# Block counts on ScalarE beside VectorE's histogram, and the first ranks made two blocks at a time

## Chip, cores and metric

The kernel runs on one core of a Trainium2 chip. The metric is the device time of one execution in microseconds (us). Before the change it is 6723.85 us, the median of 3 runs (6722.99 to 6726.43).

## What is computed

Four graph layers over one graph of 6250 nodes and 100000 edges, each followed by a residual and a layer norm:

```python
edge_index = jnp.stack([src, dst])
x = _layernorm(x + _L0_gnn_ref(x, edge_index, ...), axis=-1)      # two hops, then two matrices
x = _layernorm(x + _L1_gnn_ref(x, edge_index, ...), axis=-1)      # hypergraph convolution
x = _layernorm(x + _L2_gnn_ref(x, edge_weight, src, dst), axis=-1)
x = _layernorm(x + _L3_gnn_ref(x, edge_index, edge_attr_64, ...), axis=-1)   # attention over edges
```

The change touches only what comes ahead of the layers: the kernel counts the edges of each destination node (for `deg`) and sorts the edges by the block of their source node. There are 49 blocks of 128 nodes (`NB` = 49). For each edge its rank in that order is needed, and for this the number of edges of each source block in each of the 128 partitions (`cnt`).

## The kernel before

The program is a row of phases. Each phase (`phase`, L66) is a block in which the five engines run side by side, ordered by semaphores, and it ends with a barrier of all engines. What a phase takes is so what its slowest engine takes. The first three phases matter here.

**prepare** (L118). SyncE's queue loads the edge lists, the node rows and the weights, then fills the table `bucketed_edges` in HBM with 52 transfers of 544 KB (L158). VectorE makes the index tables. `m.shi` is the source block of each of the 784 edges that a partition holds; its name in the trace is `start_t`. Then comes a loop of 49 iterations (L278). An iteration first counts one source block: L280 compares all 784 values of `shi` with the block's number and adds up the hits into one column of `m.cnt`. Then it makes the one-hot rows of 16 edge columns in two halves of 8: L285 the high part of the destination (one instruction for 8 columns), L289 the low part (one for each column). TensorE adds them up as a histogram in PSUM (L328). After the loop VectorE makes `deg` (L293), ScalarE its root (L175), VectorE the reciprocal (L295) and the scaled node rows (L298), which SyncE's queue stores (L161). This store and the fill of L158 must have landed before the phase ends.

**starts** (L767, `bucket_starts`). TensorE sums `cnt` over the partitions (L798, L799). VectorE makes from it where each block starts, and then the ranks of the first 112 edge columns of each partition (`CHUNKS[1]` = 7 * 16) in `rank_columns` (L749). It takes the 49 blocks one after the other: a mask (L756), a running sum over it that starts at the block's present position in each partition, `m.first` (L758), a copy of the sum to `m.rank` where the mask holds (L760), and a copy of its last column back to `m.first` (L761). Each of them waits for the one that it reads from, and the iteration's last wait is for all four.

**bucket** (L806). GpSimd scatters the edges by their ranks (L863, 784 indirect DMAs), 16 columns at a time. ScalarE makes the indices (L844) and copies three values for each edge (L847); it may begin with the first 112 columns at once and waits for the further ranks, which VectorE makes meanwhile with `rank_columns` for 224 and 448 columns. Then VectorE makes a second histogram, with the same shapes as the first one but without a count (L881, L885, L898).

`hold` (L87) is a wait followed by a NOP.

Of the kernel before, what the change touches and what calls it, by code (L numbers as in the profile page):

```python
# [7 lines left out]
I32 = mybir.dt.int32  # L8
ALU = mybir.AluOpType
# [4 lines left out]
P = 128  # L14
N, D = 6250, 128
E, DE = 100000, 64
M = 2500
# [5 lines left out]
NT = NI * U  # L23
# [37 lines left out]
assert Q3 == 2 * G and U3 // G % RG == 0  # L61
assert NI == NB
assert (P - 1) * NT + SPLIT * U == E and 0 < SPLIT < NI
assert M <= KW <= NB * P and (NB - 1) % CR == 0 and (NB - 1) % 2 == 0 and 3 * NB * NR <= BT and NB % GB == 0 and NPC % RING == 0 and NCH == MB


class Names:
# [47 lines left out]
def prepare(nc, m, a):  # L115
# [7 lines left out]
    whole, rest = (P - 1) * NT, E - (P - 1) * NT  # L123
    with phase(nc, "prepare", "filled loaded_edges loaded_rows counted loaded_x loaded_w iota dve hw_row consts nat transposed evacuated "
                              "diag replicated rep_used span_ready wT wT_used prefilled fill hist_ready "
                              "hist_used degree root scaled stored") as (S, block):
        FT = (CH - 1) * P
        LT = FULL - FT

# [36 lines left out]
        @block.scalar  # L166
        def _(act):
            act.dma_start(m.hwrow[:, 0:M], a.hw.rearrange("(o n) -> o n", o=1).broadcast_to([P, M])).then_inc(S["hw_row"], 16)
            act.wait_ge(S["hw_row"], 16)

            for k, dst in enumerate((m.w1T, m.w2T, m.WT)):
                act.wait_ge(S["wT"], k + 1)
                nc.scalar.copy(dst[:, :], m.ps[:, 4 + k, 0:P]).then_inc(S["wT_used"], 1)
            act.wait_ge(S["degree"], 1)
            nc.scalar.activation(m.dinv[:, :], m.deg[:, :], ACT.Sqrt).then_inc(S["root"], 1)  # L175

# [12 lines left out]
        def _(v):  # L189
# [80 lines left out]
            step(V.tensor_copy(m.dst2, rowI[1]))  # L270
            step(V.tensor_scalar(m.shigh, m.dst2, float(M), PAD, ALU.is_lt, ALU.mult))
            step(V.tensor_tensor(m.shigh, m.shigh, m.shi, ALU.add))

            v.wait_ge(S["hw_row"], 16)
            step(V.memset(m.hwrow[:, M:KW], 0.0))
            step(V.memset(m.side[:, NP:AW], 0.0))

            with v.Fori(0, NI) as i:  # L278
                b = bass.ds(i, 1)
                V.tensor_scalar(m.tabs[:, 0:NT], m.shi, m.iota[:, b], None, ALU.is_equal, ALU.add, accum_out=m.cnt[:, b]).then_inc(S["counted"], 1)  # L280
                for h in range(2):

                    v.wait_ge(S["hist_used"], i * 2 + h + 1)
                    cols = bass.ds(i * U + h * HALF, HALF)
                    V.tensor_tensor(m.ohhi[:, h * HALF:(h + 1) * HALF, :],  # L285
                                    m.dhi[:, cols].unsqueeze(2).to_broadcast([P, HALF, NB]),
                                    m.iota[:, 0:NB].unsqueeze(1).to_broadcast([P, HALF, NB]), ALU.is_equal).then_inc(S["hist_ready"], 1)
                    for k in range(HALF):
                        V.tensor_scalar(m.ohlo[:, h * HALF + k, :], m.iotab[:, :], m.dlo[:, bass.ds(i * U + h * HALF + k, 1)],  # L289
                                        None, ALU.is_equal).then_inc(S["hist_ready"], 1)  # L290
                v.wait_ge(S["counted"], i + 1)
            v.wait_ge(S["hist_used"], 2 * NI + 3)
            V.tensor_scalar(m.deg[:, :], m.ps[:, 7, 0:NB], 1.0, None, ALU.add).then_inc(S["degree"], 1)  # L293
            v.wait_ge(S["root"], 1)
# [467 lines left out]
        v.wait_ge(S["ranked"], i * 4 + (done * 4 * NB + 4))  # L762


def bucket_starts(nc, m):


    with phase(nc, "starts", "dve cnt_in_psum ends ends_in_psum ranked") as (S, block):
        @block.vector
        def _(v):  # L770
            V, step = nc.vector, chain(v, S["dve"])
            v.wait_ge(S["cnt_in_psum"], 2)

            step(V.tensor_copy(m.bI[:, :], m.ps[:, 0, 0:NB]))
            step(V.tensor_scalar(m.bF[:, :], m.bI[:, :], float(P - 1), None, ALU.add))
            step(V.tensor_copy(m.bI[:, :], m.bF[:, :]))
            step(V.tensor_scalar(m.bI[:, :], m.bI[:, :], 7, None, ALU.arith_shift_right))
            step(V.tensor_copy(m.bF[:, :], m.bI[:, :]))
            step(V.tensor_tensor_scan(m.ends[:, :], m.ones[:, 0:1].to_broadcast([P, NB]), m.bF[:, :], 0.0, ALU.mult, ALU.add))
            step(V.tensor_tensor(m.bF[:, :], m.ends[:, :], m.bF[:, :], ALU.subtract))  # L780
            step(V.tensor_copy(m.fac[:, :], m.bF[:, :]))
            step(V.tensor_scalar(m.bF[:, :], m.bF[:, :], float(P), -1.0, ALU.mult, ALU.add))
            step(V.tensor_tensor(m.first[:, :], m.bF[:, :], m.ps[:, 1, 0:NB], ALU.add))

            for col, u, sh in ((2, U, 4),):
                step(V.tensor_scalar(m.small[0:1, col:col + 1], m.ends[0:1, NB - 1:NB], float(u - 1), None, ALU.add))
                step(V.tensor_copy(m.smallI[0:1, col:col + 1], m.small[0:1, col:col + 1]))
                step(V.tensor_scalar(m.smallI[0:1, col:col + 1], m.smallI[0:1, col:col + 1], sh, None, ALU.arith_shift_right))
            V.tensor_copy(m.bF[:, :], m.ends[:, :]).then_inc(S["ends"], 1)
            v.wait_ge(S["ends_in_psum"], 2)  # L790
            step(V.tensor_copy(m.bstart[0:NB, :], m.ps[0:NB, 3, 0:1]))
            step(V.tensor_copy(m.endp[0:NB, :], m.ps[0:NB, 2, 0:1]))
            step(V.tensor_scalar(m.rank[:, :], m.tF[:, 0:NT], float(DUMP), None, ALU.add))
            rank_columns(nc, v, m, S, 0, 0)

        @block.tensor
        def _(pe):
# [946 lines left out]
```

## Time and profile before

| | |
|---|---|
| time, median of 3 runs | 6723.85 us |
| time of the profiled execution | 6730.24 us |
| its span in the trace | 6728.5 us |
| TensorE busy | 4012.2 us (60%) |
| VectorE busy | 3279.4 us (49%) |
| GpSimd busy | 3044.2 us (45%) |
| ScalarE busy | 1187.3 us (18%) |
| prepare | to about 356 us |
| starts | about 356 to 446 us |
| bucket begins | 446.8 us |

The busy shares are means over some thirty phases. Since every phase ends in a barrier, they tell little of one phase: which engine or transfer ends it must be read from its own stretch of the trace.

### The profile page before, as it was taken

To read this page: it belongs to the slowest core of one execution; us is meant where nothing else is said; L and a number is where in the kernel's file an instruction comes from. 1 tells how busy PE (TensorE), PEld (TensorE's weight loads), DVE (VectorE), ACT (ScalarE), POOL (GpSimd) and SP (SyncE) were. 2 spreads that over 40 slices of the span, in tenths; PEclk is the share of its full clock that TensorE was granted. 3 is DMA by queue.
4 is the path that set the end of the run, shared out by engine and by line. 5 is a ranking of instruction groups with operands and counts; after the bars stand their busy time and mean duration, and the time that the engine had idled before them with its cause. 6 is when DMAs were issued, how large, how long until landed. Compare 5 with 4: busy or idle time off the path is not lost. (4 is left out here: it accounts for less than half of the span.)

```text
span 6728.5 us, 101449 instructions
## 1 busy us (share of the span) xinstructions
PE 4012.2 (60%) x17222; PEld 2420.5 (36%) x17251; DVE 3279.4 (49%) x11280; ACT 1187.3 (18%) x3845; POOL 3044.2 (45%) x3024
## 2 busy tenths in 40 slices
PE   2600510002676777876877999566666567777777
PEld 1300300000111112434454456343443357666665
DVE  5967920003555555443122033544444557788783
ACT  0000000000111110001012022100000156666652
POOL 0027877770000003874750000377777447777750
PEclk9999999999656557888975999555555589999995
DMA  8611112217111114655732856111111234444450
GB/s 128 88 37 48 40 50 54 54 51 23 70 62 70 62 70 157 204 178 173 258 107 100 311 192 199 44 53 52 53 52 53 46 108 130 125 126 127 124 103 19
DMA packets 717405, 673.00 MB, mean 100 GB/s; under 512 B 487624, under 2 KB 616377, under 8 KB 698166
## 3 DMA queue, kind: packets, MB, share of 16 engines
q1 hardware_dynamic: 607526, 442.47, 23.8%
q0 software_dynamic: 109568, 227.77, 12.2%
q14 instruction: 152, 1.25, 0.1%
q10 hardware_dynamic: 144, 1.28, 0.1%
q8 instruction: 15, 0.25, 0.0%
HBM read 528.30 MB, written 142.96 MB: 100 GB/s over the span
## 5 line engine op out<-in xcount | busy, mean ns | idle before, releaser
L488 POOL DMA_INDIRECT gathered<-node_table,idx x576 | 621.3, 1079 | 1174.9 <-ACT idx L476 1015.5
L863 POOL DMA_INDIRECT bucketed_edges<-edge_rows,idx x784 | 822.9, 1050 | 681.6 <-issue 663.3
L1329 POOL DMA_INDIRECT gathered<-node_table_xq,idx x832 | 798.5, 960 | 377.3 <-issue 225.0
L360 POOL DMA_INDIRECT gathered<-node_table,idx x816 | 771.0, 945 | 285.4 <-issue 203.3
L375 PE MATMUL ps<-onehots,gathered 128*128 128x128 f32 x1632 | 642.5, 500 | 422.0 <-DMA gathered<-node_table,idx 421.4
L1239 PE MATMUL ps<-onehots 128*128 128x512 bf16 x1152 | 573.3, 571 | 263.6 <-DVE onehots L1266 253.6
L435 PE MATMUL ps<-gathered,junk 128*128 128x512 f32 x1182 | 608.1, 623 | 90.2 <-DMA gathered<-edge_counts 90.0
L375 PEld LDWEIGHTS ps<-onehots,gathered 128*128 128x128 f32 x1632 | 408.1, 312 | 656.4 <-DMA gathered<-node_table,idx 656.1
L1157 PE MATMUL ps<-tabs,ones 49*128 49x416 f32 x4 | 3.1, 938 | 707.1 <-DVE tabs L1112 707.1
L1264 DVE TENSOR_SCALAR onehots<-iota_b,side_rows,bF 128x128 bf16<-128x128 bf16 x722 | 227.2, 315 | 396.9 <-issue 207.3
L971 POOL MEMSET agg<- 128x6400 f32 x4 | 21.7, 5432 | 848.5 <-ACTq L81 848.5
L1418 PE MATMUL ps<-Wh,attend_slots 128*128 128x128 f32 x1664 | 357.7, 299 | 47.8 <-issue 44.1
L504 PEld LDWEIGHTS ps<-onehots,gathered 128*128 128x128 f32 x1152 | 223.2, 210 | 446.0 <-DMA gathered<-node_table,idx 251.5
L539 DVE TENSOR_TENSOR onehots<-ps,off_t 128x512 f32<-128x512 f32 x156 | 107.2, 691 | 534.0 <-PE ps L504 530.5
L1239 PEld LDWEIGHTS ps<-onehots 128*128 128x128 bf16 x1152 | 90.6, 108 | 731.0 <-DVE onehots L1266 729.2
L504 PE MATMUL ps<-onehots,gathered 128*128 128x128 f32 x1152 | 264.4, 316 | 145.6 <-DMA gathered<-node_table,idx 141.2
L1112 DVE TENSOR_SCALAR tabs<-tile_iota_i,endp 49x832 f32<-49x832 f32 x1 | 0.6, 645 | 706.2 <-PEq L84 706.2
L1419 PE MATMUL ps<-side_rows,attend_slots 128*128 x1664 | 343.1, 290 | 0.0
L393 DVE TENSOR_TENSOR onehots<-ps,off_t 128x512 f32<-128x512 f32 x208 | 143.9, 692 | 400.1 <-PE ps L375 400.0
L1266 DVE TENSOR_SCALAR onehots<-junk,side_rows 128x1024 bf16<-128x1024 f16 (+1 forms) x722 | 312.2, 432 | 30.0
L1218 ACT COPY gathered<-ps 128x512 f32<-128x512 f32 x245 | 133.9, 588 | 971.4 <-PE ps L1242 971.4
L898 PE MATMUL ps<-gathered 128*128 128x49 bf16 x784 | 123.5, 222 | 304.2 <-DVE gathered L885 294.0
(358 smaller groups left out, 7719.2 us busy)
## 6 DMA issues: line engine op xcount, KB each, us to landing
gathered<-edge_counts SPq DMA_DIRECT2D x99, 1280.0 KB
edge_counts<-gathered SPq DMA_DIRECT2D x49, 1280.0 KB
gathered<-edge_counts SPq DMA_DIRECT2D x56, 896.0 KB
bucketed_edges<-edge_rows SPq DMA_DIRECT2D x52, 544.0 KB, 12.1
edge_rows<-bucketed_edges SPq DMA_DIRECT2D x208, 128.0 KB
gathered<-edge_counts SPq DMA_DIRECT2D x48, 512.0 KB
side_rows<-edge_counts SPq DMA_DIRECT2D x48, 512.0 KB
gathered<-node_table,idx POOLq DMA_INDIRECT x1392
```

Source lines behind the costliest of these rows:

```text
L360: nc.gpsimd.indirect_dma_start(g[:, k, :], None, table, bass.IndirectOffsetOnAxis(m.idx[:, k:k + 1], 0)).then_inc(S["landed"][k], 16)
L375: last = nc.tensor.matmul(m.ps[:, q, e * P:(e + 1) * P], g[:, k, :], m.oh[:, k, :], start=True, stop=True)
L435: mm = nc.tensor.matmul(m.ps[:, k, :], m.junk[:, j, :], row_piece(m, j, k), start=first, stop=False)
L488: nc.gpsimd.indirect_dma_start(g[:, k, :], None, a.table, bass.IndirectOffsetOnAxis(m.idx[:, k:k + 1], 0)).then_inc(S["landed"][k], 16)
L504: last = nc.tensor.matmul(sums[q % NS], g[:, k, :], m.oh[:, k, :], start=e == 0, stop=e == G - 1)
L863: nc.gpsimd.indirect_dma_start(a.bucketed, bass.IndirectOffsetOnAxis(m.idx[:, k:k + 1], 0), m.erow[:, k, :], None).then_inc(S["scattered"] ...
L1239: last = T.matmul(m.ps[:, k, :], ohs[h], ohd[h][:, (k - k0) * KB:(k - k0 + 1) * KB], start=False, stop=False)
L1264: V.tensor_scalar(ohs[h], m.iotab[:, :], m.meta[:, bass.ds(t + h, 1), 2], m.bF[:, bass.ds(b, 1)], ALU.subtract, ALU.is_equal)
L1266: V.tensor_scalar(ohd[h][:, 0:w], iotaK[:, 0:w], m.meta[:, bass.ds(t + h, 1), 1], -float(k0 * KB), ALU.subtract, ALU.is_equal).then_inc(S[ ...
L1329: nc.gpsimd.indirect_dma_start(g[:, k, :], None, a.table2, bass.IndirectOffsetOnAxis(m.idx[:, k:k + 1], 0)).then_inc(S["landed"][s], 16)
L1418: T.matmul(out, m.eT[:, 2 * h + e // 2, :], m.Wh[:, e % 2, :], start=True, stop=False)
L1419: last = T.matmul(out, m.ohT[:, G * h + e, :], m.side[:, bass.ds(start[e], P)], start=False, stop=True)
```

## The change

ScalarE makes the 49 counts, in two passes for each block over one of two buffers in `m.side`: the square of (block number minus `shi`), which is 0 where the edge belongs to the block and at least 1 elsewhere, and then Relu(1 - square), whose sum is the count. It starts when `shi` is there (the new semaphore `blocks`). The count and its wait leave VectorE's loop. In the phase starts, the first 112 columns' ranks are made for two blocks in one iteration: two masks, two running sums, then copy and `first` for the one and the other, in two buffers each; the 49th block is left for the end. The ranks of the later parts are as before.

```diff
+            act.wait_ge(S["blocks"], 1)
+            act.sem_inc(S["counted"], 2)
+            apart = [m.side[:, k * NT:(k + 1) * NT] for k in range(2)]
+            with act.Fori(0, NB // 7) as i:
+                b0 = act.snap(i * 7)
+                for j in range(8):
+                    if j < 7:
+                        act.wait_ge(S["counted"], b0 + max(j + 1, 2))
+                        nc.scalar.activation(apart[j % 2], m.shi, ACT.Square, scale=-1.0, bias=m.iota[:, bass.ds(b0 + j, 1)]).then_inc(S["apart"], 1)
+                    if j >= 1:
+                        act.wait_ge(S["apart"], b0 + j)
+                        nc.scalar.activation(apart[(j - 1) % 2], apart[(j - 1) % 2], ACT.Relu, scale=-1.0, bias=m.ones[:, 0:1],
+                                             accum_out=m.cnt[:, bass.ds(b0 + (j - 1), 1)]).then_inc(S["counted"], 1)
+            act.wait_ge(S["counted"], NB + 2)
             act.wait_ge(S["degree"], 1)
             nc.scalar.activation(m.dinv[:, :], m.deg[:, :], ACT.Sqrt).then_inc(S["root"], 1)
...
             step(V.tensor_tensor(m.shigh, m.shigh, m.shi, ALU.add))
+            v.sem_inc(S["blocks"], 1)
...
             with v.Fori(0, NI) as i:
-                b = bass.ds(i, 1)
-                V.tensor_scalar(m.tabs[:, 0:NT], m.shi, m.iota[:, b], None, ALU.is_equal, ALU.add, accum_out=m.cnt[:, b]).then_inc(S["counted"], 1)
                 for h in range(2):
...
-                v.wait_ge(S["counted"], i + 1)
...
+def rank_columns_by_two(nc, v, m, S):
+
+    V, n = nc.vector, CHUNKS[1]
+    mask, cum = ([t[:, k * n:(k + 1) * n] for k in range(2)] for t in (m.tabs, m.cum))
+
+    def ranks(b0, count, base):
+        b = [bass.ds(b0 + k, 1) for k in range(count)]
+        for k in range(count):
+            V.tensor_scalar(mask[k], m.shi[:, 0:n], m.iota[:, b[k]], None, ALU.is_equal).then_inc(S["ranked"], 1)
+        for k in range(count):
+            hold(v, S["ranked"], base + (k + 1))
+            V.tensor_tensor_scan(cum[k], m.ones[:, 0:1].to_broadcast([P, n]), mask[k], m.first[:, b[k]], ALU.mult, ALU.add).then_inc(S["ranked"], 1)
+        for k in range(count):
+            hold(v, S["ranked"], base + (count + 1 if k == 0 else 2 * count + 1))
+            V.copy_predicated(m.rank[:, 0:n], mask[k].bitcast(I32), cum[k]).then_inc(S["ranked"], 1)
+            V.tensor_copy(m.first[:, b[k]], cum[k][:, n - 1:n]).then_inc(S["ranked"], 1)
+        v.wait_ge(S["ranked"], base + 4 * count)
+    with v.Fori(0, NB // 2) as i:
+        ranks(v.snap(i * 2), 2, v.snap(i * 8))
+    ranks(NB - 1, 1, 4 * (NB - 1))
...
-            rank_columns(nc, v, m, S, 0, 0)
+            rank_columns_by_two(nc, v, m, S)
```

In the instruction lists that follow, ISA, REGISTER_ALU and the branches belong to the sequencer; a semaphore in brackets is waited for ahead of that row. Semaphores that a later phase takes over keep the name of their first owner.

ScalarE in prepare, from the copies of the transposed weights to the root of `deg`, before:

```order
L173 ACT_TABLE_LOAD [waits prepare_wT]
L173 COPY w1T<-ps 128x128 [waits prepare_hw_row]
L173 COPY w2T<-ps 128x128 [waits prepare_wT]
L173 COPY WT<-ps 128x128 [waits prepare_wT]
L175 ACT_TABLE_LOAD
L175 ACTIVATE dinv<-deg 128x49 [waits prepare_degree]
```

And now, the end of the new loop over 7 blocks and what follows it:

```order
L182 ISA [waits prepare_counted]
L182 ACTIVATE side_rows<-start_t,iota 128x784
L184 ISA
L185 ISA [waits prepare_apart]
L185 ACTIVATE side_rows,cnt<-side_rows,ones 128x784
L184 ISA
L185 ISA [waits prepare_apart]
L185 ACTIVATE side_rows,cnt<-side_rows,ones 128x784
L177 REGISTER_ALU
L177 COMPARE_AND_BRANCH
L189 ACT_TABLE_LOAD [waits prepare_degree]
L189 ACTIVATE dinv<-deg 128x49 [waits prepare_counted]
```

The loop holds activations alone; the load of the table for the root stands behind it, and it now carries the wait for `deg`, which the root alone carried before.

VectorE in starts, the loop over the 49 blocks, before:

```order
L754 ISA
L756 TENSOR_SCALAR tabs<-start_t,iota 128x112
L757 ISA
L758 ISA [waits prepare_loaded_x]
L758 SCALAR_TENSOR_TENSOR gathered<-ones,first,tabs 128x112
L89 ISA
L760 COPY_PREDICATED rank_t<-tabs,gathered 128x112 [waits prepare_loaded_x]
L761 ISA
L761 COPY first<-gathered 128x1
L762 ISA
L754 REGISTER_ALU [waits prepare_loaded_x]
L754 COMPARE_AND_BRANCH
```

And now, the same loop over 24 pairs, up to the first block's copies:

```order
L785 TENSOR_SCALAR tabs<-start_t,iota 128x112
L785 ISA
L785 TENSOR_SCALAR tabs<-start_t,iota 128x112
L89 ISA
L788 ISA [waits prepare_loaded_x]
L788 SCALAR_TENSOR_TENSOR gathered<-ones,first,tabs 128x112
L89 ISA
L788 ISA [waits prepare_loaded_x]
L788 SCALAR_TENSOR_TENSOR gathered<-ones,first,tabs 128x112
L89 ISA
L791 COPY_PREDICATED rank_t<-tabs,gathered 128x112 [waits prepare_loaded_x]
L792 ISA
```

Behind each mask there was its own running sum and nothing else to do meanwhile; now the other block's mask or sum stands between a sum and its copy. What follows in the loop, not shown, is the copy to `first` of the first block, the two copies of the second block (L791, L792) behind one more hold, and the wait for all eight.

## Rows read from the trace of the kernel before

**Rows 1.** Windows: us; PE, PEld, DVE, ACT, POOL busy; PEclk, DMA share, GB/s

```profile
280.00:300.00 20.00, 11.52 (x69) 7.01 (x68) 20.00 (x88) 0.00 (x0) 0.00 (x0) 1.00 0.00 0
...
343.00:356.00 13.00, 0.00 (x0) 0.00 (x0) 0.00 (x0) 0.00 (x0) 0.00 (x0) 1.00 0.86 247
```

**Rows 2.** Timeline of prepare's loop, VectorE: start us, us, instruction, xcount

```profile
122.05 1.03 DVE L280 TENSOR_SCALAR_CACHE_REDUCE tabs<-start_t,iota 128x784 f32<-128x784 f32 x1
...
122.99 0.57 DVE L285 TENSOR_TENSOR gathered<-gathered,iota 128x392 bf16<-128x392 f32 x1
123.47 1.39 DVE L289 TENSOR_SCALAR gathered<-iota_b,gathered 128x128 bf16<-128x128 bf16 x8
...
126.55 1.03 DVE L280 TENSOR_SCALAR_CACHE_REDUCE tabs<-start_t,iota 128x784 f32<-128x784 f32 x1
```

**Rows 3.** Sources of both histogram loops: ns min/median/max, first to last start

```profile
L280 DVE TENSOR_SCALAR_CACHE_REDUCE tabs<-start_t,iota x49: 1025/1031/1033, 113.0 to 329.4; 128x784 f32<-128x784 f32 x49
L289 DVE TENSOR_SCALAR gathered<-iota_b,gathered x784: 250/257/259, 114.5 to 333.8; 128x128 bf16<-128x128 bf16 x196
L881 DVE TENSOR_TENSOR gathered<-ew_t,iota x98: 552/564/581, 700.0 to 872.6; 128x392 bf16<-128x392 f32 x98
L885 DVE TENSOR_SCALAR gathered<-iota_b,off_t x784: 238/255/493, 700.5 to 874.3; 128x128 bf16<-128x128 bf16 x196
```

**Rows 4.** Timeline of prepare's end: start us, us, instruction, [idle before, releaser]

```profile
334.56 0.21 DVE L293 TENSOR_SCALAR deg<-ps 128x49 f32<-128x49 f32 x1 [0.53 <-PE ps L332]
334.80 0.24 ACT L175 ACTIVATE dinv<-deg 128x49 f32<-128x49 f32 x1 [251.15 <-DVE deg L293]
...
342.52 0.37 SPq L161 DMA_DIRECT2D node_table<-t_nodes  x1
```

**Rows 5.** Source L158, the fill: issue ns min/median/max, first to last start

```profile
L158 SPq DMA_DIRECT2D bucketed_edges<-edge_rows x52: 399/3552/4394, 78.3 to 256.7; - x52
```

**Rows 6.** Groups of ScalarE by form: us busy, mean ns of one, idle before

```profile
L1364 ACT ACTIVATE attend_slots<-junk,ones 128x512 bf16<-128x512 f32 x208 | 150.1, 721 | 23.0
L1084 ACT ACTIVATE gathered<-x_nodes 128x3200 f32<-128x3200 f32 x4 | 11.5, 2869 | 2.6 <-DVE x_nodes L1065 2.6
L1084 ACT ACTIVATE gathered<-x_nodes 128x3072 f32<-128x3072 f32 x4 | 11.1, 2762 | 41.1 <-DVE x_nodes L1065 41.1
L1380 ACT ACTIVATION_READ_ACCUMULATOR probs<-scores,negm 128x1 f32 x104 | 19.4, 187 | 0.0
```

**Rows 7.** Timeline of ScalarE at a table load: start us, us

```profile
5463.20 1.28 ACT L1379 ACT_TABLE_LOAD   x1
5464.50 0.20 ACT L1379 ACTIVATE c<-dif 128x1 f32<-128x1 f32 x1
```

**Rows 8.** Timeline of VectorE in starts: one block's ranks, the next mask

```profile
363.99 0.28 DVE L756 TENSOR_SCALAR tabs<-start_t,iota 128x112 f32<-128x112 f32 x1 [0.44 <-DVE first L761]
364.40 0.45 DVE L758 TENSOR_TENSOR_SCAN gathered<-ones,first,tabs 128x112 f32<-128x112 f32 x1
364.95 0.28 DVE L760 COPY_PREDICATED rank_t<-tabs,gathered 128x112 f32<-128x112 int32 x1
365.15 0.15 DVE L761 COPY first<-gathered 128x1 f32 x1
365.71 0.28 DVE L756 TENSOR_SCALAR tabs<-start_t,iota 128x112 f32<-128x112 f32 x1 [0.41 <-DVE first L761]
```

**Rows 9.** Source L761 in starts; ScalarE's waits: us in total, times, longest

```profile
L761 DVE COPY first<-gathered x49: 146/147/150, 363.4 to 445.8; 128x1 f32 x49
ACT idx L844 <- DMA bucketed_edges<-edge_rows,idx: 1006.4, 96, 15.8
...
ACT idx L844 <- PEq L84: 111.8, 1, 111.8
```

**Rows 10.** Windows of later phases, columns as in rows 1

```profile
1820.00:1980.00 160.00, 112.75 (x267) 23.03 (x270) 89.27 (x239) 21.13 (x39) 0.00 (x0) 0.57 0.16 66
...
4060.00:4220.00 160.00, 160.00 (x773) 103.95 (x773) 48.74 (x83) 40.95 (x70) 0.00 (x0) 1.00 0.55 180
```

More of the change, by code:

```diff
@@ L63 @@
 assert (P - 1) * NT + SPLIT * U == E and 0 < SPLIT < NI
-assert M <= KW <= NB * P and (NB - 1) % CR == 0 and (NB - 1) % 2 == 0 and 3 * NB * NR <= BT and NB % GB == 0 and NPC % RING == 0 and NCH == MB
+assert M <= KW <= NB * P and (NB - 1) % CR == 0 and (NB - 1) % 2 == 0 and 3 * NB * NR <= BT and NB % 7 == 0 and 2 * CHUNKS[1] <= NT and NB % GB == 0 and NPC % RING == 0 and NCH == MB
 class Names:
@@ L125, in prepare @@
                               "diag replicated rep_used span_ready wT wT_used prefilled fill hist_ready "
-                              "hist_used degree root scaled stored") as (S, block):
+                              "hist_used degree root scaled stored blocks apart") as (S, block):
         FT = (CH - 1) * P
```

## Prediction, made before the changed kernel ran

> **What bounds the kernel here.** The whole-kernel shares say little, so I began with the windows over the first 446 us, then read the groups by source line, the timelines of the loops, and the waits.
>
> In prepare, VectorE is busy for every microsecond of the histogram loop while ScalarE does nothing and TensorE is busy for 58% [rows 1]. The loop is VectorE's: each of 49 iterations lasts 4.50 us (122.05 to 126.55), and 0.94 us of it (122.05 to 122.99) passes between the start of the count and that of the next instruction [rows 2]. Behind the loop hangs a chain with one engine at a time: `deg`, root, reciprocal, scaled rows, and the store of L161 from 342.52 [rows 4]. The only other thing that this phase waits for is the fill of `bucketed_edges`: its last transfer is issued at 256.7 [rows 5], and from 280 to 300 us the DMA engines move nothing [rows 1].
>
> In starts, the ranks of part 0 are a chain on VectorE alone. Blocks follow each other at 1.72 us (363.99 to 365.71) [rows 8], and the last one's copy starts at 445.8 [rows 9]. The bucket phase begins at the barrier behind it: that is ScalarE's single wait of 111.8 us ahead of L844. Later ScalarE waits at L844 only for scattered edges, never for ranks [rows 9].
>
> So both edits work on stretches that nothing else covers, with a barrier behind each, and what they save is saved at the end, unless something else in prepare is uncovered or a later stage answers to the shift.
>
> **The counts.** Removed from VectorE: 49 counts. The price is measured twice. By the timeline, 0.94 to 0.95 us each. By a loop that stands in the same trace without the count, in the bucket phase, with the same shapes: 174.3 us from its first start to its last (700.0 to 874.3) against 220.8 us for prepare's (113.0 to 333.8) [rows 3]. The difference is **46.5 us**, and it already holds the branch, the register work and TensorE's pace. The wait on `counted` costs nothing in either.
>
> Added on ScalarE: 98 passes over 784 columns. No such shape is in the trace. From 512 columns (721 ns) and 0.84 ns for each further column (107 ns for 128 more, 2762 to 2869) a pass is 0.95 us, and reading the sum is 0.19 us [rows 6]. A block is then 2.09 us; with 0.1 us for the wait of a pass for the one before, 2.2 us. 49 of these are 108 us: from about 113 us, when the loop starts, to 221. VectorE's loop would end at 113.0 + 174.6 = 287.6, so 67 us of cover are left, and I cost this at nothing. If the cover were gone, each microsecond of ScalarE behind 287.6 would be one of the kernel. The bounds for a block: 1.9 us (each pass overlapping the next by 0.09) and 3.1 us (half as slow again); neither reaches the cover's end.
>
> The fill: it must land before the phase ends, and it has about 20 us in hand. The store of L161 would start at 342.5 - 46.5 + 1.3 = 297.3, behind the last fill, whose engines are idle from 280 at the latest. It costs nothing, but the reserve is used: a further 30 us taken from VectorE here would be partly lost.
>
> The table load: before, ScalarE loaded the root's table at leisure. Now the load stands behind the loop, and it, not the root, carries the wait for `deg`. It falls into the chain of [rows 4]. The one load inside a run of work goes from 5463.20 to the next start at 5464.50 [rows 7], so **+1.3 us**. Bounds: 0 (if the load runs ahead of the wait after all) and 2.6 (paid twice). The Trainium skill, "ScalarE: Activation LUTs", What ACT_TABLE_LOAD costs, adds a drain of about 1380 ns to the 1283 ns of the load, 2.66 us in all. By that the sum would be 1.4 us smaller in its gain. The row shows 1.30 us from start to start with no drain behind or ahead, and the sum goes by the row.
>
> **The ranks.** One block today: mask to sum 0.41 us, sum to copy 0.55, copy to `first` 0.20, `first` to the next mask 0.56, together 1.72 [rows 8]. Three of these steps hold a wait for the instruction just before (0.13, 0.10 and 0.41 us of idling). The third, copy to `first`, holds none: there the second starts 0.20 us after the first, which lasts 0.28; they overlap by nearly 0.09 us. Now a pair, from its first mask: second mask at 0.20; first sum at 0.41 (it waits for the first mask alone, as today); second sum at 0.82, halfway between the 0.77 of an overlap and the 0.86 of none, since no row shows a sum followed without a wait; first copy at 1.18 and its `first` at 1.37; the second copy waits for the first to be done, 0.38 behind its start, 1.56; its `first` at 1.75; next mask 0.56 later, at 2.31. Two blocks today are 3.43 (48 steps at 1.717, from 363.40 to 445.8, make 82.4 us [rows 9]). That is 1.13 us for each pair, and 24 pairs give **27 us**. The 49th block stays as it is. Bounds: 10 us if only the loop's idle 0.41 us is saved once in each pair (24 x 0.41), 31 us if the sums overlap and the second copy has no wait of its own. I take 27, since each of its steps but one has a row.
>
> **Sum.** -46.5 + 1.3 - 27 = -72.2 us. The profiled execution took 6730.24 us (span 6728.5 and 1.7 around it), so it would take 6658.0. It stands 6.4 us above the median of the runs, 6723.85, and the median moves to about 6651.6; I say 6652, which is 1.1% less. About 0.2% (13.4 us) is what a measurement of this kernel can tell from no change.
>
> **Rivals.**
> *No overlap on VectorE.* If an instruction starts only when the one before has left the engine, a pair is: second mask at 0.28, first sum 0.56, second 1.01, first copy 1.46, `first` 1.74, second copy 1.89, `first` 2.17, next mask 2.73. That saves 0.70 x 24 = 17 us, and the time is 6662. The Trainium skill, "VectorE: DVE Perf Modes", The DRAIN you can't avoid, says of chained operations that the next does not start until the pipe empties, semaphores or not; by that rule pairing buys only the waits. The step from copy to `first` speaks against it (0.20 us behind an instruction of 0.28) [rows 8]; the untested sum speaks for some of it. Chance 0.14.
>
> *Only the loop's idling is saved.* Holds and register work in front of each new instruction eat the rest; 10 us in place of 27, 6669. The hold in front of today's copy costs 0.10 us all told, which speaks against it. Chance 0.04.
>
> *Slower: the clock.* Later phases answer to TensorE's clock, which was granted at 0.57 on the average in the count phase (between the levels of 1.2 and 2.4 GHz) and at 1.00 in the stretch from 4060 to 4220 us, in which TensorE is busy all the time [rows 10]. All of this comes 72 us earlier now, behind a shorter and denser start. If the grant of that busy stretch and the like one before it, 320 us, fell to half for more than 86 us, the change would be slower; if for half of them, the time is 6652 + 160 = 6812. For it: the level has fallen elsewhere under less work. Against it: three runs within 3.4 us, and the histogram's density is that of the bucket phase, which ran at 1.00. A shift by some 10 us either way is as likely as not, and the range has room for it. Chance of a slower kernel 0.03.
>
> *The counts don't hide.* If each of the 98 passes brought a table load of 1.30 us, a block would be 4.8 us and ScalarE done at 113 + 235 = 348, 60 us behind VectorE's loop: 6712, no measurable change. It decides from 3.6 us a block, and gives all back at 5.0. The instruction list has one load, behind the loop. Chance 0.02.
>
> **Chances and range.** The forecast 0.77, no overlap 0.14, idling alone 0.04, slower clock 0.03, counts uncovered 0.02. Faster 0.95, same 0.02, slower 0.03. The range goes from 6639 (27 turned to 31, and 9 us for the later stages) to 6672 (10 us from the ranks, the load at 2.6, and 2 of the later stages): it takes in the first two rivals and leaves the others out.
>
> **What the profile after would show.** Right: the first one-hot to the last in prepare at about 174 us; ScalarE busy in it for about 100 us and done near 221; a table load of 1.28 us between `deg` and the root; ranks of part 0 stepping by 2.3 us a pair; the bucket phase beginning at 446.8 - 72 = 374.6; GpSimd's scatter as long as before. Wrong: a VectorE loop over 176 us (ScalarE in its way), a ScalarE end behind 287, a pair over 2.6 us, DMA still busy with the fill when the store starts, or later phases longer than before by more than some microseconds.

## The result, and the profile of the changed kernel

| | median (lowest to highest) us, runs |
|---|---|
| before, in the same series | 6727.2 (6721.93 to 6770.42), 12 |
| changed | 6695.95 (6679.31 to 6727.43), 12 |
| ratio, 95% interval | 0.9948 [0.9926, 0.9971] |
| profiled execution of the changed kernel | 6687.46, span 6685.7 |
| forecast | 6652 (6639 to 6672) |

The changed kernel is faster, by 31 us between the medians and 35 by the ratio. The forecast was 72, and its range did not hold the time. About half of the expected gain is missing. I first looked for it where the gain should arise.

The sources of prepare's two loops and of the ranks, changed kernel (ns min/median/max, first to last start):

```profile
L182 ACT ACTIVATE side_rows<-start_t,iota x49: 932/948/950, 112.4 to 206.7; 128x784 f32<-128x784 f32 x49
L185 ACT ACTIVATE side_rows<-side_rows,ones x49: 931/932/935, 114.1 to 208.5; 128x784 f32<-128x784 f32 x49
L185 ACT ACTIVATION_READ_ACCUMULATOR side_rows<-side_rows,ones x49: 184/186/189, 114.9 to 209.3; - x49
L298 DVE TENSOR_TENSOR gathered<-gathered,iota x98: 553/560/571, 112.8 to 285.3; 128x392 bf16<-128x392 f32 x98
L302 DVE TENSOR_SCALAR gathered<-iota_b,gathered x784: 242/249/259, 113.3 to 287.0; 128x128 bf16<-128x128 bf16 x196
L792 DVE COPY first<-gathered x49: 140/146/148, 318.1 to 376.1; 128x1 f32 x48, 128x1 f32<-128x1 f32 x1
```

VectorE's histogram goes from 112.8 to 287.0, 174.2 us where it was 220.8 [rows 3]. ScalarE needs 2.0 us a block and is done at 209.5, with 78 us in hand. The ranks' last copies span 58.0 us (318.1 to 376.1) where they spanned 82.4 [rows 9].

The end of prepare, timeline (start us, us, instruction, idle before and its releaser), answering to [rows 4]:

```profile
287.74 0.21 DVE L305 TENSOR_SCALAR deg<-ps 128x49 f32<-128x49 f32 x1 [0.53 <-PE ps L344]
288.03 1.28 ACT L189 ACT_TABLE_LOAD   x1 [78.53 <-DVE deg L305]
289.32 0.24 ACT L189 ACTIVATE dinv<-deg 128x49 f32<-128x49 f32 x1
...
297.04 0.37 SPq L161 DMA_DIRECT2D node_table<-t_nodes  x1
```

`deg` comes 46.8 us earlier, the table load waits for it and takes 1.3 us on the path, and the store starts 45.5 us earlier. The fill is not in its way: from 260 to 280 us the DMA engines are busy for 23% (it was issued by 257.7).

One pair of ranks on VectorE, timeline, answering to [rows 8] (x2 is two instructions shown as one):

```profile
321.97 0.47 DVE L785 TENSOR_SCALAR tabs<-start_t,iota 128x112 f32<-128x112 f32 x2 [0.55 <-DVE first L792]
322.45 0.79 DVE L788 TENSOR_TENSOR_SCAN gathered<-ones,first,tabs 128x112 f32<-128x112 f32 x2
323.16 0.26 DVE L791 COPY_PREDICATED rank_t<-tabs,gathered 128x112 f32<-128x112 int32 x1
323.33 0.14 DVE L792 COPY first<-gathered 128x1 f32 x1
323.53 0.29 DVE L791 COPY_PREDICATED rank_t<-tabs,gathered 128x112 f32<-128x112 int32 x1
323.72 0.15 DVE L792 COPY first<-gathered 128x1 f32 x1
324.40 0.47 DVE L785 TENSOR_SCALAR tabs<-start_t,iota 128x112 f32<-128x112 f32 x2 [0.54 <-DVE first L792]
```

A pair takes 2.43 us where 2.31 was forecast. The two sums, with no wait between them, take 0.79 us together though one alone takes 0.45: they overlap, as the step from copy to `first` had it. What came out longer is the stretch from `first` to the next mask, 0.54 us idle in place of 0.41. That this is a matter of the loop's place, and not of the term, shows below.

So the front part did what was forecast, but for 2.5 us. What comes behind it did not. Below, how much earlier (-) or later (+) a place is reached than in the profiled execution of before, for the kernel changed and the experiments that follow. "Scatter" is the start of the last scatter of the bucket phase (1512.0 in before), "count" the first and last matmul of the count phase (1633.5, 2598.1) and "attention" the first and last start of ScalarE's 128x128 pass there (5445.7, 6527.6).

| kernel | `deg` | bucket begins | scatter | count first | count last | attention first | last | end |
|---|---|---|---|---|---|---|---|---|
| changed | -46.8 | -69.7 | -69.2 | -69.1 | -58.1 | -57.5 | -43.4 | -42.8 |
| e1 changed again | -46.6 | -69.4 | -62.9 | -63.0 | -51.8 | -49.8 | -3.7 | -1.4 |
| e2 counts only | -46.5 | -45.1 | -42.2 | -42.2 | -42.3 | -41.1 | -21.1 | -20.8 |
| e3 ranks only | -0.1 | -24.3 | -24.6 | -24.6 | -13.4 | -20.7 | -7.8 | -6.9 |
| e4 changed, delayed | -46.4 | +16.5 | +36.2 | +36.5 | +34.2 | +47.0 | +15.1 | +14.7 |
| e5 changed + 94 | -46.4 | -72.1 | -59.7 | -59.5 | -61.8 | -61.7 | -95.4 | -93.8 |
| e6 before + 109 | +0.3 | +0.3 | +16.2 | +16.3 | +14.0 | +19.7 | -12.1 | -12.0 |
| e7 before + 15 | -0.5 | +4.8 | +9.0 | +9.0 | +20.2 | +16.1 | +46.2 | +46.8 |
| e8 changed + 241 | -47.1 | -72.7 | -69.4 | -69.5 | -68.9 | -73.4 | -80.8 | -80.5 |
| e12 changed + 78 | -46.3 | -71.9 | -73.8 | -73.8 | -75.6 | -75.6 | -111.9 | -107.6 |

Each row is one execution, set against one execution of before from the first series. The chip of e1 to e4 ran before at a median of 6748.72 us, 21 above the first series, so the lengths of phases compare better there than the ends do; and the execution of e6 is the slowest of its six. A number behind "changed" or "before" is how many cheap instructions were added, as told below.

In the changed kernel 69 us are still in hand when the count phase begins, 1200 us behind the last edited instruction. Then 11 us go in the count phase and 14 in attention. Both phases' code is the same as before. The rows of their longest loops (source view, columns as above) show the same durations over a longer stretch:

```profile
L1273 PE MATMUL ps<-onehots x1152: 378/608/635, 1564.4 to 2540.0; 128*128 128x512 bf16 x192
L1394 ACT ACTIVATE junk<-iota,off_now x832: 384/386/404, 5388.2 to 6484.2; 128x128 f32<-128x128 f32 x167
```

In before the same two rows are:

```profile
L1239 PE MATMUL ps<-onehots x1152: 379/608/634, 1633.5 to 2598.1; 128*128 128x512 bf16 x192
L1360 ACT ACTIVATE junk<-iota,off_now x832: 384/386/404, 5445.7 to 6527.6; 128x128 f32<-128x128 f32 x167
```

The count phase lasts 975.6 us in place of 964.6, the attention 1096.0 in place of 1081.9. No instruction there is slower; they stand further apart. The waits view of the changed kernel (engine, line, waited for: us in total, times, longest) has a candidate, idle time of VectorE that no semaphore ends ("issue"). With it stands the same instruction's wait for TensorE:

```profile
DVE onehots L1298 <- issue: 155.3, 436, 1.5
DVE onehots L1298 <- PE ps L1273: 253.0, 286, 1.7
DVE mnew L1483 <- issue: 82.0, 24, 4.0
DVE hid L1526 <- issue: 11.2, 26, 1.2
```

In before these are:

```profile
DVE onehots L1264 <- issue: 207.3, 516, 1.6
DVE onehots L1264 <- PE ps L1239: 189.6, 206, 1.7
DVE mnew L1449 <- issue: 82.4, 24, 3.8
DVE hid L1492 <- issue: 2.1, 3, 1.4
```

The `onehots` rows are the count phase's: its "issue" fell by 52 us and its wait for TensorE rose by 63, so these rows do not say by themselves what made the phase longer. The row of `hid`, in attention, grew by 9 us. That of `mnew` is as large in both, but it is a strange one: 24 times 3.4 us, in a loop whose body repeats 25 times. It stands at the loop's head. Before's timeline of VectorE there, the last instruction of one pass and the first of the next:

```profile
5906.29 0.16 DVE L1524 TENSOR_REDUCE mx<-scores 128x1 f32<-128x8 f32 x1
...
5909.92 0.28 DVE L1449 TENSOR_REDUCE mnew<-ps 1x1 f32<-1x128 f32 x1 [3.47 <-issue]
```

That made a theory of the place of an instruction. The Trainium skill, "Runtime: NRT & Kernel Launch", Instruction fetch mechanics, says that an engine holds its instructions in two pages of 256 and that a taken branch to a target outside them makes it fetch before it goes on. VectorE's program has 2080 instructions in before and 2095 in the changed kernel, so everything behind the edits stands 15 places further on (3 places back between the two edits), while the jump back of attention spans more than 300. ScalarE's program grew too, from 982 to 1030. By that rule the price of a loop depends on where its instructions stand, and an edit upstream can change it without touching it. The rivals: later phases answer to their start time (by TensorE's clock, say), or one of the two edits itself does harm later.

### The profile page after: what moved, and what is told of

Read it like the earlier page. It is cut to its first block and busy times, and to the rows that moved or that the text cites. A ratio compares the mean times of both kernels' runs of the same rounds, so it can differ in the third digit from the quotient of the medians.

```text
span 6685.7 us, 101583 instructions
## 1 busy us (share of the span) xinstructions
PE 4010.1 (60%) x17222; PEld 2431.3 (36%) x17251; DVE 3222.0 (48%) x11182; ACT 1279.9 (19%) x3992; POOL 3045.9 (46%) x3024
## 6 DMA issues: line engine op xcount, KB each, us to landing
bucketed_edges<-edge_rows SPq DMA_DIRECT2D x52, 544.0 KB, 12.1
```

## The experiments

The first four ran on one chip, together with 35 runs of before (median 6748.72).

**The changed kernel once more**, unedited, for how far its executions agree in each phase.

> The changed kernel once more, to see what stays and what scatters. Both theories: the first one-hot to the last in prepare 174 us, pairs of ranks at 2.43 us, the bucket phase's scatter 70.8 us earlier than before, the lists phase 69.1 us earlier. Theory A (the later phases that answer to TensorE's clock take their time by when they start, and the front's gain is whole): the count phase and the attention phase differ from the first profile's by several us each, and the total scatters between about 6680 and 6730. Theory B (the change itself makes these two phases slower): they lose 11 and 14.6 us again, within 2 us, and the total is 6685 to 6700.

Measured: 6705.66 us (6691.4 to 6730.58, 12 runs), ratio 0.9936 [0.9917, 0.9956]. The result repeats: a loss of 11.2 us in the count phase, and a gain in all of some 43 us here, from 30 to 56 by the interval. In attention the profiled execution took 1128.0 us, 32 more than the first one of the same program. So in attention single executions scatter, and a difference of 14 us between two profiles there says nothing by itself.

**The counts alone:**

```diff
-            rank_columns_by_two(nc, v, m, S)
+            rank_columns(nc, v, m, S, 0, 0)
```

> The counts on ScalarE alone, the ranks block by block as before. Front: 45.5 us earlier at the store, 46 at the start of the bucket phase. Theory A: the count and attention phases shift by an amount that is neither 0 nor in proportion, either sign, up to some 30 us together; total 6665 to 6710. Theory B with ScalarE's passes as the cause: again about 26 us given back, total about 6703 to 6708 with little scatter.

Measured: 6715.59 us (6702.62 to 6743.62, 12 runs), ratio 0.9956 [0.9937, 0.9974], a gain of 33 us by the medians. The bucket phase begins 45.1 us earlier, which is the term of the sum to the microsecond. The count phase has its old length (-42.2 at its start, -42.3 at its end): the 11 us do not belong to the counts. VectorE's program here is 3 instructions shorter than in before, and ScalarE's is as long as in the changed kernel. The total lies above both expectations, on a chip that is slower than the one they were made from.

**The ranks alone** (the count back in VectorE's loop; ScalarE's loop and the semaphore `blocks` gone):

```diff
-            v.sem_inc(S["blocks"], 1)
...
+                b = bass.ds(i, 1)
+                V.tensor_scalar(m.tabs[:, 0:NT], m.shi, m.iota[:, b], None, ALU.is_equal, ALU.add, accum_out=m.cnt[:, b]).then_inc(S["counted"], 1)
+                v.wait_ge(S["counted"], i + 1)
```

> The ranks by pairs alone, the counts in VectorE's loop as before. Front: 24 us earlier at the start of the bucket phase, 0 at the store. Theory A: total 6724 - 24 and up to 30 us either way, by what the two phases do. Theory B with ScalarE as the cause: 6700, nothing given back.

Measured: 6741.45 us (6723.34 to 6779.07, 12 runs), ratio 1.0003 [0.9981, 1.0025]. The pairs save 24.3 us where they stand, and at the end the ratio shows nothing of it (its interval leaves room for a gain of 13 us). The 11.2 us of the count phase are here. Either pairs do harm later, or the 18 more instructions of VectorE do.

**The changed kernel, held up ahead of the ranks**, so that the later phases begin near before's times, with the shift in time gone and the edits kept:

```diff
+            for _ in range(94):
+                step(V.memset(m.tabs[:, 0:NT], 0.0))
             rank_columns_by_two(nc, v, m, S)
```

> The changed kernel with 94 chained fills of 784 columns on VectorE (about 0.74 us each, 69.6 us) ahead of the ranks in the phase starts, so that every later phase starts when it did before. Theory A: the later phases take what they take in the kernel before, and the total is that of before within 10 us (6715 to 6735) with its narrow scatter. Theory B (the change slows later phases whenever they start): the front's gain is gone and the loss of 26 us stays, 6745 to 6755.

Measured: 6739.6 us (6733.12 to 6745.24, 12 runs), ratio 0.9985 [0.997, 0.9999]. The delay came out at 86.2 us, 0.92 us for each fill, so the bucket phase begins 16.5 us later than in before. Yet at the end only 15 us are lost, for attention took 1050.0 us, 32 less than in before, and the 24 idle stretches at its head are gone from the waits. The median is 9 us below that of before on this chip. Since the start came later and not earlier than in before, and the phase became shorter than in either, start time alone does not explain it. But the kernel also had 94 more instructions of VectorE. The next runs separate the two.

The next four ran on one chip, with 17 runs of before (median 6733.93). Here the added instructions are fills of one column, which stand in a wait of some 63 us of VectorE for the weights early in prepare, and cost no time themselves. In the changed kernel 94 of them make 109 places with the 15 of the change:

```diff
+            for _ in range(94):
+                step(V.memset(m.chi[:, 0:1], 0.0))
             for n in range(2 * CH):
```

> The changed kernel with 94 one-column fills of an unused tile on VectorE, in the 63 us in which it waits for the weights: nothing starts later, but every later instruction of VectorE stands 94 places further in its stream, as in e4_delay70. Theory L (the later phases answer to where a loop stands in VectorE's stream: a jump back over more instructions than are at hand waits for them): no idle time ahead of the attention loop's first instruction (24 stalls, 82 us in the changed kernel, gone in e4_delay70), attention 1050 us from the first to the last ScalarE start instead of 1096 to 1128, and the total 80 to 110 us below before. Rival S (the later phases answer to when they start, and e4_delay70 was fast because it was late): the stalls may go, but attention takes 1096 us or more, total 30 to 45 us below before.

Measured: 6636.44 us (6635.24 to 6643.36, 5 runs), ratio 0.9856 [0.9839, 0.9874]. That is 97 us faster than before, and some 60 faster than the changed kernel in the first series, with nothing added but fills in idle time. `deg` and the start of the bucket phase are where the changed kernel has them; attention lasts 1048.2 us. Its head in the waits by source (the instruction, then what ended the idle time before it: us, times):

```profile
L1485 DVE TENSOR_REDUCE mnew<-ps x104: 278/278/280, 5400.3 to 6453.4; 1x1 f32<-1x128 f32 x104
...
  PE ps L1444: 37.8, 104
```

and the same in the changed kernel without fills:

```profile
L1483 DVE TENSOR_REDUCE mnew<-ps x104: 278/278/280, 5403.4 to 6504.1; 1x1 f32<-1x128 f32 x104
...
  issue: 82.0, 24
  PE ps L1442: 29.0, 80
```

All 104 now wait 0.36 us for TensorE, and none for issue. At the jump back, the timeline of e5 reads:

```profile
5849.57 0.16 DVE L1560 TENSOR_REDUCE mx<-scores 128x1 f32<-128x8 f32 x1
...
5850.09 0.28 DVE L1485 TENSOR_REDUCE mnew<-ps 1x1 f32<-1x128 f32 x1 [0.36 <-PE ps L1444]
```

3.47 us of idling have become 0.36.

**The same place for before:** 109 fills in before's kernel, which puts its later loops where those of e5 are.

```diff
+            for _ in range(109):
+                step(V.memset(m.chi[:, 0:1], 0.0))
```

> The kernel before with 109 such fills, so that VectorE's attention loop stands where e5_after_pad94 and e4_delay70 have it. Theory L: the 24 stalls of 3.4 us are gone, attention about 1050 us, total 15 to 35 us below before, and e5_after_pad94 stands some 70 us below this one: the change's own gain, whole. Rival S: total as before within 6 us.

Measured: 6706.42 us (6704.71 to 6718.28, 6 runs), ratio 0.9957 [0.9942, 0.9973]. The fills alone make before faster by 27 us. Its attention has no stall either:

```profile
L1451 DVE TENSOR_REDUCE mnew<-ps x104: 278/278/279, 5482.0 to 6535.2; 1x1 f32<-1x128 f32 x104
...
  PE ps L1410: 37.8, 104
```

Between e5 and e6, which differ by the change alone and have their later loops at equal places, stand **70.0 us** (6706.42 - 6636.44). That is the change's own gain, where the sum had 72.2. (Equal places means VectorE's; ScalarE's program is 48 instructions longer in e5 than in e6. In what follows its length decides nothing: the stalls are there and gone with either length, and so is the loss in the count phase.)

**The change's shift without the change:** 15 fills in before's kernel.

```diff
+            for _ in range(15):
+                step(V.memset(m.chi[:, 0:1], 0.0))
```

> The kernel before with 15 such fills, so that VectorE's later instructions stand at the places that they have in the changed kernel, and start when they did. Theory L: the count phase takes 11 us longer than in before (from the first to the last TensorE start 975.6 instead of 964.6), and the total is 10 to 35 us above before. Rival S: count phase unchanged within 2 us, total as before.

Measured: 6769.21 us (6748.82 to 6794.1, 12 runs), ratio 1.0046 [1.0025, 1.0068], 35.3 us slower than before. This is the missing half: -70.0 + 35.3 = -34.7, and the changed kernel's ratio gave 35 (0.0052 x 6727). That it closes so neatly is luck: e7's interval runs from 17 to 46 us, and its 12 times lie in two groups, 6749 to 6761 and 6777 to 6794, between which the median falls. In its profiled execution the loss is 4.8 us up to the bucket phase, 4 in it, 11.2 in the count phase and 30 in attention (4 are won back between those two); in attention single executions differ by as much, as e1 showed. Its count phase, from the source view:

```profile
L1241 PE MATMUL ps<-onehots x1152: 379/607/634, 1642.5 to 2618.3; 128*128 128x512 bf16 x192
L1362 ACT ACTIVATE junk<-iota,off_now x832: 384/386/406, 5461.8 to 6573.8; 128x128 f32<-128x128 f32 x167
```

975.8 us, 11.2 more than before, what the changed kernel (975.6), its repetition and the ranks alone show. And the waits view has the changed kernel's row at `hid` in attention:

```profile
DVE onehots L1266 <- issue: 144.3, 424, 1.7
...
DVE mnew L1451 <- issue: 78.7, 24, 4.6
...
DVE hid L1494 <- issue: 10.1, 25, 0.5
```

Neither an earlier start nor pairs of ranks nor work on ScalarE is in this kernel.

**A full 256 places:** 241 fills with the 15 of the change. If the pages are of 256 instructions, every loop stands in its page as in before.

```diff
-            for _ in range(94):
+            for _ in range(241):
```

> The changed kernel with 241 such fills: with its own 15 more instructions VectorE's later ones stand 256 places behind those of before. Theory L with pages of 256 instructions (the Trainium skill, Runtime: NRT & Kernel Launch, Instruction fetch mechanics): the count phase is as in before (964.6 us within 2), the 24 stalls are there as in before, and the total is 65 to 75 us below before. Without such a page: the count phase takes any time between. Rival S: total 30 to 45 us below before, as the changed kernel.

Measured: 6655.7 us (6649.69 to 6702.13, 6 runs), ratio 0.9897 [0.9871, 0.9922], a gain of 78 us by the medians and 69 by the ratio, about the forecast's 72; the time lies inside its range. The waits are before's again:

```profile
DVE onehots L1300 <- issue: 211.1, 519, 1.7
...
DVE mnew L1485 <- issue: 81.1, 24, 3.6
```

The count phase lasts 965.2 us as in before (964.6), the row of 10 us at `hid` is gone, and the 24 stalls are there as in before. This agrees with a period of 256 places; no other period was tried. It starts 70 us earlier than before does, so the start time is not what lengthens the count phase.

The last four ask how wide the zone without stalls is. The three first ran with 17 runs of before (median 6742.54), the fourth on another chip with 9 (6738.83). An estimate from the two pages of 256 that the Trainium skill states ("Runtime: NRT & Kernel Launch", Instruction fetch mechanics): the trace shows some 358 instructions in one pass of the loop, which fit in two pages from 2 x 256 - 358 = 154 of the 256 places. So moving on by 30 or 60 places from e5 might well stay in the zone.

```diff
+            for _ in range(154):
```

> The changed kernel with 154 fills, 60 places further than e5_after_pad94. In e5 the ranks of 448 columns took 0.25 us more in each of 49 iterations, as would a small loop that lies across a border between two stretches of the stream. Theory L: the attention loop stays without its stall (it needs three stretches of 256 only for some 100 of the 256 places), and the border has left the rank loops: attention 1048 us, bucket phase 10 to 13 us shorter than e5's, total 6620 to 6636 where before is 6734. If the place of the loops were not what counts: as the changed kernel, 6690 to 6705.

Measured: 6660.97 us (6655.86 to 6695.37, 7 runs), ratio 0.9869 [0.9844, 0.9895]. The stalls are there, where none was expected:

```profile
DVE mnew L1485 <- issue: 78.5, 24, 4.0
```

```diff
+            for _ in range(124):
```

> The changed kernel with 124 fills, 30 places further than e5_after_pad94. Theory L: no stall ahead of the attention loop, attention 1048 us; the loops that cross a border in e5 no longer do, another may; total 6620 to 6645 where before is 6734.

Measured: 6672.82 us (6663.3 to 6700.19, 6 runs), ratio 0.9895 [0.9865, 0.9924]. Again the expectation of none fell: 24 stalls, 80.1 us.

```diff
+            for _ in range(60):
```

> The changed kernel with 60 fills, 34 places short of e5_after_pad94, to see where the stall goes. Theory L: either no stall and a total of 6625 to 6645, or all 24 stalls of 3.4 us (nothing between the two) and a total of 6655 to 6700 where before is 6734.

Measured: 6712.21 us (6698.94 to 6733.43, 12 runs), ratio 0.9952 [0.9935, 0.9969]. All 24 stalls, 79.2 us, as one of the two outcomes had it, but the time lies above the 6700 given for it.

```diff
+            for _ in range(78):
```

> The changed kernel with 78 fills, 16 places short of e5_after_pad94, between e11 (60, all stalls) and e5 (94, none). In e5 the ranks of 448 columns took some 0.25 us more in each of 49 iterations; 16 places less would carry the border out of that loop into the histogram loop behind it, which nothing waits for. Theory L: either no stall, attention about 1048 us and a bucket phase up to 13 us shorter than e5's, total 95 to 115 us below before; or all 24 stalls, total 40 to 75 below before, if the border of the attention loop falls between 78 and 94 places.

Measured: 6624.18 us (6622.03 to 6632.92, 5 runs), ratio 0.9827 [0.9805, 0.985], no stall. This is the fastest version of all, 115 us faster than before and some 70 to 80 faster than the changed kernel. Attention lasts 1045.6 us:

```profile
L1396 ACT ACTIVATE junk<-iota,off_now x832: 384/386/404, 5370.1 to 6415.7; 128x128 f32<-128x128 f32 x167
```

So the stalls are all or nothing: none at +93 and +109 places from before, all 24 at -3, 0, +15, +18, +75, +139, +169 and +256.

What the stalls are, the profiles' count of DMA traffic shows. One of the queues is marked as carrying instructions (packets, MB, share of the engines). It reads, in before and in e6:

```profile
q14 instruction: 152, 1.25, 0.1%
q14 instruction: 33, 0.26, 0.0%
```

All ten kernels with stalls have 152 to 155 packets there, the four without have 33 or 34. The difference arises in attention: between the first and the last start of ScalarE's pass the queue moves 126 or 127 packets in the ones and 7 in the others, about 5 packets of 8 KB more for each of the 24 jumps back. So at a stalling place each jump back has instructions loaded again. In the count phase the same queue moves 1 or 2 packets in every run, whether the phase lasts 962 or 976 us: its 11 us are not such loads.

Short loops have places too. The waits view of e5 has a row in the bucket phase:

```profile
DVE gathered L772 <- DVE tabs L770: 11.6, 49, 0.5
```

The same row of 11.6 us is in e4 and e6, and in no other run. It is the loop that makes the ranks of 448 columns. One iteration in e5:

```profile
502.60 0.45 DVE L770 TENSOR_SCALAR tabs<-start_t,iota 128x448 f32<-128x448 f32 x1 [0.55 <-DVE first L775]
...
503.28 1.15 DVE L772 TENSOR_TENSOR_SCAN gathered<-ones,first,tabs 128x448 f32<-128x448 f32 x1 [0.23 <-DVE tabs L770]
...
505.78 0.45 DVE L770 TENSOR_SCALAR tabs<-start_t,iota 128x448 f32<-128x448 f32 x1 [0.55 <-DVE first L775]
```

and in the changed kernel:

```profile
500.08 0.45 DVE L768 TENSOR_SCALAR tabs<-start_t,iota 128x448 f32<-128x448 f32 x1 [0.41 <-DVE first L773]
...
500.67 1.15 DVE L770 TENSOR_TENSOR_SCAN gathered<-ones,first,tabs 128x448 f32<-128x448 f32 x1
```

An iteration takes 3.18 us there against 2.95 here: 0.23 more, 49 times 11 us, for the same instructions at other places. The bucket phase up to its last scatter lasted 12 us longer than in before in e5 and 16 longer in e6, and I took this row for the reason. That is not shown: ScalarE waits there for scattered edges and never for these ranks, in e5 as in before, and the phase was 8 and 9 us longer in e9 and e11 too (6 in e1), where the row is absent.

A short loop whose price does reach the end is that of the first ranks. The waits of a pair's first mask, in the changed kernel and in e5:

```profile
DVE tabs L785 <- DVE first L792: 12.8, 24, 0.9
DVE tabs L787 <- DVE first L794: 10.0, 24, 0.5
```

These are 0.54 and 0.43 us a pair. At the places of e5, e8 and e12 a pair takes 2.32 us, and the bucket phase begins 72.1, 72.7 and 71.9 us earlier than in before. In e7 the blocks of before's own loop follow each other with 0.53 us of idling in place of 0.41, and the phase begins 4.8 us later.

## Why the prediction was wrong

**The counts** were right: -46.5 forecast, -46.8, -46.6 and -46.5 measured at `deg` (changed, e1, e2). ScalarE needed 2.0 us a block where I took 2.2, within the bounds, and it hid as forecast.

**The table load** was right: 1.3 us on the path, behind the wait for `deg`. With the drain that the Trainium skill states ("ScalarE: Activation LUTs", What ACT_TABLE_LOAD costs) it would have been 2.66; the load and what follows show 288.03 to 289.32, 1.29 us, as [rows 7] did.

**The fill** cost nothing, as forecast.

**The ranks** were forecast at 27 us and gave 24.3 (alone) and 24.2 (store to bucket phase). The missing 3 us are not the term's: they are the idling of 0.54 us from `first` to the next mask, which is 0.43 at other places, where the front comes 72 us earlier as the sum has it. The rival *no overlap on VectorE* fell at the row that decides it, two sums in 0.79 us; it had 17 us.

**The step that failed** is the sentence "what they save is saved at the end, unless something else in prepare is uncovered or a later stage answers to the shift". I had a later stage answer to the shift in time, by TensorE's clock, and gave it 10 us either way. What they answer to is the shift in place: the change makes VectorE's program 15 instructions longer, and that alone costs before's kernel 35.3 us by the medians, 17 to 46 by the interval (e7). At equal places the change gives 70.0 us (e5 against e6), or 78 where the later loops are back in before's places by a full period (e8). The sum was 72.2. It lacked a term of some +35 for the places, to which no work in the diff corresponds. In the changed kernel's profiled execution 2.5 us of it fall to the first ranks, 11 to the count phase and 14 to attention; only the first two repeat from execution to execution. The rival *slower: the clock* fell with the same runs, for e7 has the loss without the earlier start, and e8 has the earlier start without most of the loss; the mean granted clock hardly moves (0.805 in before, 0.803 changed, 0.801 in e7, 0.800 in e5, which is faster by 97 us). The sign was in the trace of before: 82.4 us of idling at "issue" ahead of one line of attention stand in its waits.

What stays open: by what mechanism 15 places make the count phase 11.2 us longer and a short loop slower (a loop across a page's border would fit, but was not isolated, and no more instructions are loaded there); why the zone without stalls is narrower than the count of pages gives; and why the executions of kernels with stalls spread over 30 to 50 us (6679 to 6727 for the changed kernel) while those without spread over 8 to 14 (6635 to 6643 in e5, 6705 to 6718 in e6). Before's attention took 32 to 36 us longer than that of the kernels without stalls. The stalls themselves are 82.4 - 8.7 (24 waits for TensorE of 0.36 us in their place), 74 us, so about half of them is covered by other work. The counts alone (e2), 3 places back, lose 20 us in the attention of the profiled execution; that is within the scatter of e1 and was not settled.

## What to carry to other kernels

A saving at the front of a kernel is worth its sum only if the loops behind it keep their places in the engines' programs: count how many instructions an edit adds ahead of long loops, and compare variants at equal places (adding cheap instructions in an idle stretch to make them so). Idle time put down to "issue" ahead of the first instruction of a loop, once for each jump back, is a cost that can be got rid of by moving the loop: here 78 one-column fills in a wait of VectorE were worth about as much as the change itself (some 70 to 80 us). Look for it before the edits, not after.

## What was not expected of the hardware

- A jump back over some 350 instructions of VectorE costs 3.4 us of idling (82.4 us in 24), all 24 times or never, by the loop's place: none at +93 and +109 places, all at the eight other places tried. The queue of instructions moves some 120 packets of 8 KB more in the attention of the kernels that stall. The rule of the two pages in the Trainium skill ("Runtime: NRT & Kernel Launch", Instruction fetch mechanics) fits the stalls and agrees with the one run at +256 (e8); the estimate of the zone made from it did not fit (e9, e10).
- A loop of few instructions can cost 0.23 us more in each iteration at one place than at another (3.18 and 2.95 us, 49 iterations).
- 15 one-column fills, hidden in a wait, make a kernel of 6734 us slower by 35 us (17 to 46); 109 make it 27 us faster.
- Two running sums without a wait between them take 0.79 us where one takes 0.45, so consecutive instructions of VectorE do overlap, by about 0.1 us.
